# Wide self-attention on one core: probabilities turned in 32x32 blocks and spread through DRAM, with work moved to GpSimd and ScalarE

## The reference, cut to what matters

```python
q = (x @ Wq).reshape(B, N, h, dh).transpose(0, 2, 1, 3) * scale
kv = x @ Wkv
k, v = (kv[..., :dh], kv[..., dh:])
sim = jnp.einsum('bhid,bjd->bhij', q, k)
...
sim = sim + bias.transpose(2, 0, 1)[None] * bias_scale
causal = jnp.triu(jnp.ones((N, N), dtype=bool), k=1)
sim = jnp.where(causal[None, None], -jnp.finfo(sim.dtype).max, sim)
attn = jax.nn.softmax(sim, axis=-1)
out = jnp.einsum('bhij,bjd->bhid', attn, v)
out = out.transpose(0, 2, 1, 3).reshape(B, N, h * dh)
return out @ Wout + bout
```

## Time and profile before

| | us |
|---|---|
| median of 3 runs (lowest to highest) | 2314.75 (2314.67 to 2318.31) |
| the profiled execution | 2314.49 |
| its span | 2312.7 |
| TensorE busy | 2059.0 (89%) |
| VectorE busy | 1834.0 (79%) |
| ScalarE busy | 1599.4 (69%) |
| GpSimd busy | 1220.3 (53%) |

### The profile page before, as it was taken

The page is one execution under the profiler, slowest core; times in us unless marked ns, Lnnn a source line. Parts: engine busy times, 40 slices in busy tenths (PEclk is TensorE's granted clock), DMA queues, the critical chain, the costliest instruction groups (busy, mean ns, idle before and its releaser), DMA issues. The chain is left out here.

```text
span 2312.7 us, 89168 instructions
## 1 busy us (share of the span) xinstructions
PE 2059.0 (89%) x32143; PEld 1736.3 (75%) x32143; DVE 1834.0 (79%) x5229; ACT 1599.4 (69%) x4229; POOL 1220.3 (53%) x1280
## 2 busy tenths in 40 slices
PE   7999999997888862439999979999899999999997
PEld 6898898885666641227888858888688888888886
DVE  4888888876899976987777667777588888888885
ACT  1766677666888876537888858888566666666664
POOL 1333333336899963009999869999233333333332
PEclk9999999998999996758999979999999999999998
DMA  5000000001111100010000000000133333333333
GB/s 130 3 0 0 0 0 0 0 1 29 34 34 35 35 18 1 1 37 2 0 0 0 0 2 1 0 0 0 35 122 116 121 118 117 116 119 122 118 115 94
DMA packets 112238, 96.96 MB, mean 42 GB/s; under 512 B 24259, under 2 KB 103430, under 8 KB 112134
## 3 DMA queue, kind: packets, MB, share of 16 engines
q1 hardware_dynamic: 108722, 94.39, 13.5%
q10 hardware_dynamic: 3412, 1.19, 0.3%
HBM read 53.59 MB, written 41.94 MB: 41 GB/s over the span
## 5 line engine op out<-in xcount | busy, mean ns | idle before, releaser
L711 POOL TENSOR_TENSOR sa_sc<-sa_sc,sa_rs 128x1024 f32<-128x1024 f32 x64 | 122.0, 1906 | 309.0 <-DVE sa_rs L687 309.0
L1883 POOL TENSOR_TENSOR lo_qk_r<-lo_qk_ms,w_neg_half 128x20 f32<-128x20 f32 x64 | 227.0, 3547 | 22.4 <-DVE lo_qk_ms L1805 22.4
L1883 POOL TENSOR_TENSOR gl_qk_r<-gl_qk_ms,w_neg_half 128x20 f32<-128x20 f32 x64 | 226.5, 3539 | 14.4 <-DVE gl_qk_ms L1805 14.1
L487 POOL TENSOR_TENSOR xan_ve<-xan_mv,w_eps_ln 128x1 f32<-128x1 f32 x64 | 12.3, 192 | 388.8 <-DVE xan_mv L481 388.8
L921 ACT ACTIVATE xa_vx<-xa_oo 64x512 f32<-64x512 f32 x256 | 151.4, 592 | 20.2 <-PE xa_oo L822 13.9
L653 ACT ACTIVATE sa_oT<-sa_oo 128x512 f32<-128x512 f32 x128 | 69.5, 595 | 117.0 <-PE sa_oo L596 117.0
L934 ACT ACTIVATE xa_oT<-xa_oo 128x512 f32<-128x512 f32 x128 | 69.5, 594 | 115.5 <-PE xa_oo L870 115.5
L832 PEld LDWEIGHTS xa_qs<-xan_xT,late_x_wq 128*128 128x128 f32 x1024 | 124.4, 192 | 30.6 <-issue 30.6
L1026 POOL TENSOR_TENSOR xa_sc<-xa_sc,xa_rs 128x1024 f32<-128x1024 f32 x64 | 122.0, 1906 | 32.8 <-DVE xa_rs L986 32.8
L560 PE MATMUL sa_qs<-san_xT,w_a_wq 128*128 128x128 f32 x1024 | 132.4, 283 | 5.0 <-DVE sa_sc L673 3.6
L881 PE MATMUL xa_yy<-late_x_wo,xa_oT 128*128 128x128 f32 x1024 | 128.4, 280 | 1.7 <-ACT xa_oT L934 1.7
(11 more groups left out here) (326 smaller groups left out, 6563.1 us busy)
## 6 DMA issues: line engine op xcount, KB each, us to landing
blocks<-xa_tb SPq DMA_DIRECT2D x64, 512.0 KB, 2.6
xa_pt<-blocks SPq DMA_DIRECT2D x256, 128.0 KB, 2.9
w_x<-in_x_dram SPq DMA_DIRECT2D x8, 512.0 KB, 7.3
ca_cx<-in_ctx_dram SPq DMA_DIRECT2D x64, 64.0 KB, 1.8
ctxT_kept<-ca_xcT SPq DMA_DIRECT2D x64, 64.0 KB, 1.6
xa_cT<-ctxT_kept SPq DMA_DIRECT2D x64, 64.0 KB, 2.5
out_dram<-xa_out SPq DMA_DIRECT2D x64, 64.0 KB, 2.0
ca_mask<-in_mask_BxSxS_ff_dram SPq DMA_DIRECT2D x64, 32.0 KB, 1.7
```

Of the source, the lines that this page charges most:

```text
L711: pool.tensor_tensor(v, v, bcast(rs[:, s, :], 2, S), ALU.mult).then_inc(prob_done, 1)
L1883: pool.tensor_tensor(qk_r[:, s, :], qk_ms[:, s, :], k["neg_half"][:, 0:NQK], ALU.pow).then_inc(sg["qk_r"], 1)
```

## The change

The probabilities are no longer turned by TensorE. VectorE turns each 32x32 block (`turn_blocks`), SyncE writes the tile to one of two DRAM buffers and reads it back in four transfers (`spread_blocks`), so that keys lie on partitions; `turn_probs` and `probsT` and two PSUM banks are gone. `attend` writes its output in another order of columns, which `outT` undoes as it copies. The subtraction of the maximum (`shift`) and the bias copy (`copy_x`) move from VectorE to GpSimd. The norm is applied by ScalarE as scale and offset; GpSimd makes the offset in two more one-column products. Lags are longer, scores and probabilities have four buffers and values eight, and the hardware loop has 8 steps in place of 4.

```diff
-        vx = sb("vx", [P, 4, 2, DH])
-        sc = sb("sc", [P, 2, 2, 8, S])
+        vx = sb("vx", [P, 8, 2, DH])
+        sc = sb("sc", [P, 4, 2, 8, S])
-        pt = sb("pt", [P, 2, 2, 4, 2, S])
+        tb = sb("tb", [P, 2, 4, 8, 32])
+        pt = sb("pt", [P, 2, 4, 2, 4, 32])
+        off, neg_mean, neg_one = sb("off", [P, 2]), sb("neg_mean", [P, 2]), sb("neg_one", [P, 1])
-        pp = [ps("pp0"), ps("pp1")]
...
+        def blocks_spread(eng, t, s, back=0):
+            if isinstance(t, int) and t - back < 0:
+                return
+            eng.wait_ge(spread[s], (t - s - back) * 32 + 64)
...
+            @block.sync
+            def _(sp):
+                def spread_blocks(t, s):
+                    after(sp, blocks_done, t)
+                    sp.dma_start(k["blocks"][s][:, :], tb[:, s, :, :, :].rearrange("p q n i -> p (q n i)")).then_inc(parked[s], 16)
+                    landed(sp, parked, t, s)
+                    for q in range(4):
+                        sp.dma_start(pt[q * 32:q * 32 + 32, s, :, :, :, :].rearrange("p a e m i -> p a (e m i)"),
+                                     k["blocks"][s].rearrange("(a p) (q n) -> q p a n", a=4, q=4)[q]).then_inc(spread[s], 16)
+
+                skewed(sp, NT, [(5, spread_blocks)])
...
-                def turn_probs(t, four):
-                    s = four % 2
-                    after(pe, prob_done, t)
-                    for e in range(2):
-                        after(pe, p_done, t, 1, per=2)
-                        for m in range(4):
-                            last = pe.transpose(pp[e][:, m * P:(m + 1) * P],
-                                                sc[:, s, e, 2 * m:2 * m + 2, :].rearrange("p a b -> p (a b)"), ident)
-                        last.then_inc(p_psum, 1)
-
...
-                    after(pe, p_done, t, per=2)
+                    blocks_spread(pe, t, s)
...
-                                last = pe.matmul(oo[u][e * 64:e * 64 + 64, :].rearrange("p (m b i) -> p m b i", m=4, b=2)[:, :, b, :],
-                                                 vx[r, four, (b + u) % 2, :], pt[r, s, e, :, b, :], start=True, stop=True)
+                                last = pe.matmul(oo[u][e * 64:e * 64 + 64, b * 256:(b + 1) * 256], vx[r, four, (b + u) % 2, :],
+                                                 pt[r, s, 2 * b:2 * b + 2, e, :, :], start=True, stop=True)
...
-                skewed(pe, NT, [(2, scores), (4, attend), (1, key_value), (1, queries), (3, turn_probs), (4, output), (0, turn)], 4)
+                skewed(pe, NT, [(3, scores), (7, attend), (2, key_value), (2, queries), (7, output), (1, turn)], 8)
...
-                def probsT(t, four):
-                    s = four % 2
-                    after(act, o_psum, t, 2)
-                    for e in range(2):
-                        act.wait_ge(p_psum, t * 2 + e + 1)
-                        act.activation(pt[:, s, e, :, :, :].rearrange("p m b i -> p (m b i)"), pp[e][:, :], ACT.Copy).then_inc(p_done, 1)
+                    act.activation(sc[:, four % 4, :, :, :], sc[:, four % 4, :, :, :], ACT.Exp).then_inc(exp_done, 1)
+
+                def apply(t, four):
+                    s = four % 2
+                    after(act, off_done, t)
+                    after(act, norm["xT_psum"], t, 2)
+                    act.activation(norm["xn"][:, s, :], tile_of(X, t), ACT.Identity, bias=off[:, s:s + 1],
+                                   scale=norm["rstd"][:, s:s + 1]).then_inc(norm["xn_done"], 1)
...
-                        act.activation(oT[:, s, u, :, :].rearrange("p m i -> p (m i)"), oo[u][:, :], ACT.Copy).then_inc(o_done, 1)
-
-                skewed(act, NT, [(4, outT), (1, key_value), (1, queries), (2, exponent), (3, probsT), (0, turned)], 4)
+                        act.activation(oT[:, s, u, :, :].rearrange("p m (a i) -> p a m i", a=4),
+                                       oo[u][:, :].rearrange("p (a m i) -> p a m i", a=4, m=4), ACT.Copy).then_inc(o_done, 1)
+
+                skewed(act, NT, [(1, apply), (7, outT), (2, key_value), (2, queries), (3, exponent), (1, turned)], 8)
...
-                def apply(t, four):
-                    norm_apply(norm, dve, tile_of(X, t), t, four % 2)
...
-                    after(dve, p_psum, t, 2, per=2)
+                    after(dve, blocks_done, t, 4)
...
-                    v = sc[:, s, :, :, :].rearrange("p e c j -> p (e c) j")
                     after(dve, biased, t, per=2)
-                    dve.tensor_reduce(mx[:, s, :], v, AX.X, ALU.max).then_inc(max_done, 1)
-                    after(dve, max_done, t)
-                    dve.tensor_tensor(v, v, bcast(mx[:, s, :], 2, S), ALU.subtract).then_inc(shifted, 1)
+                    after(dve, shifted, t, 2)
+                    dve.tensor_reduce(mx[:, s, :], sc[:, four % 4, :, :, :].rearrange("p e c j -> p (e c) j"), AX.X, ALU.max).then_inc(max_done, 1)
+
+                def turn_blocks(t, four):
+                    s = four % 2
+                    after(dve, prob_done, t)
+                    blocks_spread(dve, t, s, 2)
+                    after(dve, o_psum, t, 2)
+                    dve.transpose(tb[:, s, :, :, :],
+                                  sc[:, four % 4, :, :, :].rearrange("p e (m u) (h j) -> p (u h) (e m) j", u=2, h=2)).then_inc(blocks_done, 1)
...
                     after(dve, xb_done, t)
                     dve.tensor_tensor(tile_of(X, t), yy[:, 0:D], xb[:, s, :], ALU.add).then_inc(x_done, 1)
...
-                def copy_x(t, four):
-                    s = four % 2
-                    after(dve, x_done, t, 2)
-                    dve.tensor_tensor(xb[:, s, :], tile_of(X, t), k["a_row"][:, :], ALU.add).then_inc(xb_done, 1)
-
-                skewed(dve, NT, [(5, residual), (0, measure), (2, softmax), (0, apply), (4, copy_x), (2, sums)], 4)
+                skewed(dve, NT, [(8, residual), (3, softmax), (5, turn_blocks), (0, measure), (4, sums)], 8)
...
-                    norm_rsqrt(k, norm, pool, t, four % 2)
+                    s = four % 2
+                    after(pool, norm["mv_done"], t)
+                    pool.tensor_tensor(neg_mean[:, s:s + 1], norm["mv"][:, s, 0:1], neg_one[:, :], ALU.mult).then_inc(nm_done, 1)
+                    norm_rsqrt(k, norm, pool, t, s)
+                    after(pool, norm["rstd_done"], t)
+                    pool.tensor_tensor(off[:, s:s + 1], neg_mean[:, s:s + 1], norm["rstd"][:, s:s + 1], ALU.mult).then_inc(off_done, 1)
+
+                def shift(t, four):
+                    s = four % 2
+                    after(pool, max_done, t)
+                    v = sc[:, four % 4, :, :, :].rearrange("p e c j -> p (e c) j")
+                    pool.tensor_tensor(v, v, bcast(mx[:, s, :], 2, S), ALU.subtract).then_inc(shifted, 1)
...
-                skewed(pool, NT, [(0, rsqrt), (2, normalise)], 4)
+                def copy_x(t, four):
+                    after(pool, x_done, t, 2)
+                    pool.tensor_tensor(xb[:, four % 2, :], tile_of(X, t), k["a_row"][:, :], ALU.add).then_inc(xb_done, 1)
+
+                pool.memset(neg_one[:, :], -1.0).then_inc(minus, 1)
+                pool.wait_ge(minus, 1)
+                skewed(pool, NT, [(3, shift), (0, rsqrt), (4, normalise), (7, copy_x)], 8)
```

More of the change, by code:

```diff
@@ L533, in wide_self_attention @@
         exp_done, sum_done, inv_done, prob_done = sem("exp"), sem("row_sum"), sem("inverse"), sem("probs")
-        p_psum, p_done, o_psum, o_done = sem("probsT_psum"), sem("probsT"), sem("outT_psum"), sem("outT")
+        blocks_done, o_psum, o_done = sem("blocks_turned"), sem("outT_psum"), sem("outT")
+        parked = [sem(f"blocks_parked{s}") for s in range(2)]
+        spread = [sem(f"blocks_spread{s}") for s in range(2)]
+        off_done, nm_done, minus = sem("offset"), sem("neg_mean"), sem("minus_one")
+        def blocks_spread(eng, t, s, back=0):
+            if isinstance(t, int) and t - back < 0:
+                return
+            eng.wait_ge(spread[s], (t - s - back) * 32 + 64)
         y_psum, xb_done, x_done = sem("y_psum"), sem("x_plus_bias"), sem("x")
         with nc.Block() as block:
+            @block.sync
[8 more added lines that the diff above has]
+                skewed(sp, NT, [(5, spread_blocks)])
             @block.tensor
@@ L622, in key_value @@
                     act.activation(kT[:, s, :], misc[:, P:2 * P], ACT.Copy).then_inc(k_done, 1)
-                    after(act, o_psum, t, 4)
+                    after(act, o_psum, t, 8)
                     act.activation(vx[:, four, 0, :], misc[:, 2 * P:2 * P + DH], ACT.Copy).then_inc(v_done, 1)
@@ L638, in exponent @@
                     after(act, shifted, t)
-                    act.activation(sc[:, s, :, :, :], sc[:, s, :, :, :], ACT.Exp).then_inc(exp_done, 1)
-                def probsT(t, four):
+                    act.activation(sc[:, four % 4, :, :, :], sc[:, four % 4, :, :, :], ACT.Exp).then_inc(exp_done, 1)
+                def apply(t, four):
                     s = four % 2
```

(20 more changed lines are left out.)

## The result

The changed kernel takes 2400.03 us (median of 4 runs, 2395.96 to 2404.29) against 2314.94: 1.0364 times as long, 95% interval 1.0344 to 1.0385. It is slower, by 85 us; the forecast was 2388, with a range of 2368 to 2412. The profiled execution took 2404.29 us.

What follows compares the result with a forecast made beforehand. TensorE's queue bounds the wide self-attention before, at 7.40 us a step; after the change a loop through VectorE and GpSimd would, at 8.6. With fill and end that adds 73 us to 2314.5: 2388 us, range 2368 to 2412.

Steps and rivals of the forecast that it cites:

- The order of the queues: Wide self-attention: residual on VectorE waits for copy_x behind normalise on GpSimd, which waits for VectorE's sums; 8.6 us a step.
- The signs: VectorE waits 2.4 to 2.7 us for sa_xb ahead of residual; TensorE about 2 us a step ahead of queries.
- The size of a round: Wide self-attention: one loop through VectorE and GpSimd sums to 8.70 us, taken as 8.6, between 8.45 and 8.9.
- this case: The main forecast for wide self-attention: 8.45 to 8.9 us a step, 2379 to 2405 us in all; 77%.
- the rival of a shorter round: Wide self-attention: a step of 8.0 to 8.4 us, above 7.4, giving 2340 to 2376 us; 7%.
- The second round: Wide self-attention: residual, evictions, maximum, then GpSimd's shift, rsqrt, normalise and copy take 8.5 us, just inside the first.
- Fill and end: Wide self-attention: first residual at 75.4 us, last softmax step ending at 582.8, stage ending at 601.2 instead of 528.2.
- The clock: Wide self-attention: TensorE keeps 2.4 GHz despite 2.1 us idle in each 8.6; costed at nothing.
- the slow clock: Rival, wide self-attention: TensorE falls to 1.2 GHz, a step is 10.7 us at least, about 2510 us; 4%.
- no exclusion: Rival, wide self-attention: block turn and shift exclude each other, at worst 1.16 us a step more, 2450 us; 6%.
- The trip through DRAM: Wide self-attention: 6.9 us from turn to landing, hidden except once at the end; rival of it being late, 2%.
- TensorE as the bound: Rival, wide self-attention: VectorE does not stand behind GpSimd's copy, a step is 6.53 us, 2266 us; 4%.

Runs made afterwards that it cites:

- (1): Changed kernel with copy_x first instead of last in GpSimd's list: 2294.85 us, ratio 0.9909.
- experiment 2: Kernel before with only copy_x moved from VectorE to the end of GpSimd's list: 2486.35 us, ratio 1.0742.
- Experiments 3 to 5: Changed kernel with turn_blocks last on VectorE: 2398.63 us; with rsqrt last on GpSimd: 2399.15; with both: 2345.82.
- experiment 8: Changed kernel with TensorE's 64 steps written out without a loop: 2378.98 us, ratio 1.0280.
- Experiment 6: Kernel before with TensorE's loop in the wide self-attention at 8 steps in place of 4: 2328.20 us, ratio 1.0061.
- experiment 7: Changed kernel with TensorE's loop started on a 256-instruction boundary: 2381.07 us, ratio 1.0280.

## Why the prediction was right, point by point

**The order of the queues.** Right, and shown from both sides: moving the copy alone gives the time back (1), and the edge alone makes the kernel before slower (2). The signs came too: VectorE waited for `sa_xb` 60 times, 2.6 us each. TensorE's wait ahead of `queries` was smaller than the 2 us forecast, 60.8 us in 52 waits.

**The size of a round.** Forecast 8.6 with 8.45 to 8.9; measured 8.43 in the loop and 8.31 in the first, written-out steps, just under the lower end and between this case and the rival of a shorter round (8.0 to 8.4). By start distances in the step above: to the next start 0.21 (0.20 forecast), evictions 1.31 (1.32), maximum 1.13 (1.20), block turn 1.16 (1.16), statistics to row sums 0.54 (0.67), sums to reciprocal 1.22 (1.25), to GpSimd 0.33 (0.33), normalise 1.86 (1.90), copy to residual 0.67 (0.67). I counted overlaps of neighbours too low, by 0.17 in all. The time that I gave for the rival of a shorter round does not follow from its steps: 8.0 us a step is 58 x 0.6 = 35 us less, 2353 us and not 2340.

**The second round.** Forecast 8.5, "just inside the first, so shortening one alone would bring little". In the step above it is as long as the first, 8.43: 1.52 to the maximum, 1.30 to the shift, 1.86 and 1.22 to normalise, 1.86 and 0.67 to residual. Experiments 3 to 5 show that little meant next to nothing, and that both together count.

**Fill and end.** First residual forecast at 75.4, measured 76.5; from the residual of step 66 to the end of the stage forecast 27.0, measured 26.7 (589.10 to 615.81).

**What was missing.** The stage ends at 615.8, not at 601.2. Of these 14.6 us the fill is +1.1, the 58 steps are 512.6 in place of 498.8, and the end is -0.3. The 58 steps are -11.3 from the step's size and +25.1 from the five returns of TensorE's loop, for which my sum had no term: of the change from 4 to 8 steps in the loop the prediction said nothing. (These are times of the profiled execution, 2404.29 us; its later stages took 2 us more than before.) That the total of 2400 comes within 12 us of the forecast is in part luck, two errors of opposite sign: without the returns the changed kernel takes 2379 (experiment 8), and with my own 8.6 us a step the 25 us would have made 2413, just over the range. Experiment 6 shows that a loop of 8 steps is enough for a stop at each return, without the rest of the change, but of a third of the cost; experiment 7 shows that the second stop goes with the loop's place. The Trainium skill (Runtime: NRT & Kernel Launch, Instruction fetch mechanics) says that code is fetched ahead in straight order, in blocks of 16 KiB (256 instructions), and that a taken branch to a target outside the current window of two blocks forces a fetch before execution can go on. On the blocks the trace agrees: the packets are of 16 KiB, one ends ahead of the end of each stop, there is one fewer for each return when the loop starts on a boundary, and in straight code packets come without a stop. On the window it does not: the loop of the kernel before, 1000 products and loads, is nearly four such blocks and returned without one packet. That TensorE stands for these packets is read from their times and the edits; why a loop of 8 steps brings packets in every round and one of 4 steps none is not shown.

**The clock.** Here a step failed in part. I took the granted clock to stay at 1.00, from four microseconds of the fill. It was 0.90 between 100 and 200 us, and 0.79 between 308 and 316, where 16 query passes took 3.65 us after an idle time of 1.82: TensorE ran part of the time at 1.2 GHz. The Trainium skill (TensorE: Matmul & The Clock Gate, Part 1) says that the throttled clock is the default and activity releases it; the trace agrees with the risk that I read there and not with my cost of nothing for it. In the changed kernel it cost next to nothing: the step with the 3.65 us queries is the one of 8.43 shown above, since TensorE had 2 us to spare. In experiment 2, where the queries' copies stand ahead of the exponent in the round, the same fall cost 1.2 to 1.7 us in each of twelve steps. Had the slow clock lasted through whole steps, as the rival had it, a step would by my estimate of 10.7 us have been TensorE's.

**The other rivals.** Block turn (309.50 to 310.74) and shift (309.67 to 311.57) run side by side at 1.24 and 1.90 us, their plain durations: no exclusion. The trip through DRAM stayed hidden. TensorE as the bound came true only with the copy moved, at 6.45 us where 6.53 was the forecast of that case.

## What to carry to other kernels

When work moves between in-order queues, draw the loop that closes through them: here the first instruction of one queue's step waited for the last of the other's, which waited for the last of the first, and the sums of busy time showed nothing of it. A round of two engines that do not overlap is as long as both parts together; look for a second round of the same length before shortening one. And the longer hardware loop had a price at each return here, 1.5 to 6.4 us, that no busy time shows.

## What the runs showed of the hardware that was not expected

TensorE's code has 234 product and load instructions a step (117 products in the timeline, each with a load), 1872 in a loop of 8. At the return of such a loop TensorE stood twice, for 2.0 to 2.8 and 2.3 to 3.2 us; on a 256-instruction boundary once, for 1.1 to 2.7; in the kernel before, with loops of 1000, no such stop shows, and in straight code none. The code packets say more: while the loop of 1000 ran none came, and in every round of the loop of 1872 ten came (nine on the boundary), where the same eight steps in straight code take some 7.4 (43 packets in 391 us, at 67.5 us for eight steps). In the changed kernel the granted clock was 0.79 between 308 and 316 us, part of the time at 1.2 GHz, behind an idle time of 1.8 us, and the step's length did not change.
